# Two mixture-of-experts FFN stages: the order and the waits of GpSimd's row gathers and weight splits

## The chip, the core and the metric
One core of one Trainium2 chip runs the whole kernel as a single program. The metric is the device time in microseconds, lower being better. The time before is the median of three runs, and one further execution was recorded by the hardware profiler. Engines are named as the profile names them: PE is TensorE's matrix unit (PEld its weight load), ACT is ScalarE, DVE is VectorE, POOL is GpSimd, and SP is SyncE, which issues most of the transfers.

## The reference
The input x is 2 sequences of 1024 tokens with 128 features, 2048 tokens in all. Four blocks follow one another, each with a layer norm in front and a residual around it: a selective-scan mixer (a), an FFN, a second state-space mixer (b), and the same FFN again. The FFN is the part that matters here:

```python
def _L0_ffn_ref(x, gate_weight, shared_gate_up, shared_down, experts_gate_up, experts_down):
    E, TOPK, I = 8, 2, 938
    out = _swiglu(x, shared_gate_up, shared_down)          # every token, one shared expert
    probs = softmax(x @ gate_weight.T)
    top_p, sel = top_k(probs, TOPK)                        # two of eight experts a token
    top_p = top_p / (sum(top_p) + 1e-08)
    cw = sum(top_p[..., None] * one_hot(sel, E), axis=2)
    for e in range(E):
        out = out + cw[..., e:e+1] * _swiglu(x, experts_gate_up[e], experts_down[e])
    return out
```
`_swiglu` multiplies silu of a gate projection (128 to 938) by an up projection (128 to 938) and projects back to 128.

## The kernel before
The kernel keeps x transposed in SBUF (128 features by 2048 tokens) and writes the five engines' programs by hand: within a stage each engine runs its own list of instructions, and semaphores order them. `ffn_stage` is built twice, with the prefixes `f_` and `g_` in the names of its tiles.

**Routing.** A stage computes only what the router chose. Its 2 x 2048 (token, expert) pairs are sorted by expert and padded to 39 tiles of 128 slots (`SLOT_TILES = 39`). While the shared expert's first three quarters run on TensorE, VectorE works out which token stands in which slot (`source`), where each result row goes (`back`), its weight (`share`) and a `table` of the expert of each tile.

**Rows.** SyncE stores the normalised tokens as rows in DRAM (`xn_rows`). GpSimd fetches them, 128 rows of 512 bytes for each tile, with an indirect DMA (L1041): gather j fills `rows[:, j, :]` for tile j. Eight semaphores (`GATHERS = 8`) take turns as signals of the landing, `x_loaded[j % 8]`. After tile j has been computed, its results replace the rows, and GpSimd sends them to `token_rows` by a scatter (L1050), waiting at every fourth send until all earlier sends have landed.

**Weights.** Each expert has 1.45 MB of weights, loaded by SyncE in three transfers (L967 to L969) into one of three places of a ring (`RING = 3`). The products are computed in two parts, so GpSimd splits each expert's weights into a rounded high part and the rest: two casts (L1020, L1021) and two subtractions (L1023, L1025), which end with `w_ready`. A split waits for its load (`w_loaded`), and the load of expert n, from the fourth on, waits on SyncE for `summed`, TensorE's count that the last tile of expert n-3 is done:

```python
            for n in range(RING + 1, EXPERTS + 1):
                at = 2 * SLOT_TILES + n - RING
                first = sp.value_load(table[0:1, at:at + 1], min_val=1, max_val=SLOT_TILES)
                sp.wait_ge(summed, first + NPRE)
                load_expert(n)
```

**TensorE's tile.** `tile(j)` turns the gathered rows of tile j (L1200, "turn j" below; it waits for gather j), multiplies the products of tile j-2 by the down weights (`down_tile`, L1185 and L1188), turns the products of tile j-1 (L1167), and then, after `w_ready` of its expert, multiplies the rows by gate and up weights in two halves (L1214 to L1216). ScalarE and VectorE read each of these results from PSUM: ScalarE scales the cross term (L1361), rounds the turned products (L1356) and takes silu (L1379), VectorE multiplies (L1730), subtracts (L1699, L1703) and writes the result rows (L1709). The tiles at which one expert ends and the next begins follow from the routing table, which the inputs fix.

**GpSimd's order.** Split of expert 1; gathers 0 to 3; split 2; gathers 4 to 15; split 3; gathers 16 to 27; split 4; gathers 28 to 38; splits 5 and 6; sends 0 to 3; split 7; sends 4 to 13; split 8; the other sends; at the end four additions of returned rows. Before gather j, from the fifth on, it waits until gather j-4 has landed.

Of the kernel before, what the change touches and what calls it, by code (L numbers as in the profile page):

```python
# [8 lines left out]
F32 = mybir.dt.float32  # L9
F32R = mybir.dt.float32r  # L10
I32 = mybir.dt.int32
ALU = mybir.AluOpType
# [16 lines left out]
EXPERTS = 8  # L29
# [9 lines left out]
RING = 3  # L39
GATHERS = 8  # L40
# [14 lines left out]
class Core:  # L55
# [5 lines left out]
    def sb(self, name, shape, dt=F32, ctx=None):  # L61
        return (ctx or self.ctx).enter_context(self.nc.sbuf_tensor(name, shape, dt))
# [759 lines left out]
def ffn_stage(k, d, which, tag, cleared, ready, out=None, logs=None, following=None):  # L822
# [5 lines left out]
    nc, ps = k.nc, k.ps  # L828
# [4 lines left out]
    def sems(names):  # L833
        made = [k.sem(f"{tag}_{n}", counters) for n in names.split()]
        spent.extend(made)
        return made
# [12 lines left out]
    logit, prob, chosen, rank, spare, place = [sb(n, [P, TT, EXPERTS]) for n in  # L849
                                               "logit prob chosen rank spare place".split()]  # L850
# [24 lines left out]
    x_loaded = k.gathered  # L875

    def gathered(j):
        before = len(range(j % GATHERS, SLOT_TILES, GATHERS))
        return 16 * (j // GATHERS + 1 + which * before)

    w_loaded = sems(" ".join(f"w_loaded{b}" for b in range(RING)))
# [75 lines left out]
    def down_of(ring, place):  # L957
        return ring[:, place, 2 * GW:EW].rearrange("p (i h m) -> p i h m", i=TILES, h=2)

    with stage, nc.Block(no_gpsimd_drain=True) as block:  # L960
# [50 lines left out]
        @block.gpsimd  # L1011
        def _(pool):
            TOGETHER, SEND_FIRST, SEND_SECOND = 4, EXPERTS - 4, TT - 2

            def split_expert(n):
                place = (n - 1) % RING
                high, low, dn = ring[:, place, 0:GW], ring[:, place, GW:2 * GW], down_of(ring, place)
                raw, raw_dn = raw_ring[:, place, GW:2 * GW], down_of(raw_ring, place)
                pool.wait_ge(w_loaded[place], 48 * ((n - 1) // RING + 1))
                nc.gpsimd.tensor_copy(high, raw).then_inc(w_high, 1)  # L1020
                nc.gpsimd.tensor_copy(dn[:, :, 0, :], raw_dn[:, :, 1, :]).then_inc(w_high, 1)  # L1021
                pool.wait_ge(w_high, 2 * n - 1)
                nc.gpsimd.tensor_tensor(low, raw, high.bitcast(F32), ALU.subtract)  # L1023
                pool.wait_ge(w_high, 2 * n)
                nc.gpsimd.tensor_tensor(dn[:, :, 1, :], raw_dn[:, :, 1, :], dn[:, :, 0, :].bitcast(F32),  # L1025
                                        ALU.subtract).then_inc(w_ready, 1)

            split_expert(1)
            pool.wait_ge(k.first_row, 16)
            pool.wait_ge(rows_stored, 16 * TOP * NCH)  # L1030
            pool.wait_ge(source_ready, 1)
            for j in range(SLOT_TILES):
                if j == 4:
                    split_expert(2)
                if j == 16:
                    split_expert(3)
                if j == 28:
                    split_expert(4)
                if j >= TOGETHER:
                    pool.wait_ge(x_loaded[(j - TOGETHER) % GATHERS], gathered(j - TOGETHER))  # L1040
                nc.gpsimd.indirect_dma_start(rows[:, j, :], None, k.xn_rows,  # L1041
                                             bass.IndirectOffsetOnAxis(ap=source[:, j:j + 1], axis=0))\
                    .then_inc(x_loaded[j % GATHERS], 16)
            for n in range(RING + 2, EXPERTS - 1):
                split_expert(n)
            def send(j):
                pool.wait_ge(outs_ready, j + 1)
                if j and j % TOGETHER == 0:
                    pool.wait_ge(sent, sent_before + 16 * j)
                nc.gpsimd.indirect_dma_start(k.token_rows, bass.IndirectOffsetOnAxis(ap=back[:, j:j + 1], axis=0),  # L1050
                                             rows[:, j, :], None).then_inc(sent, 16)

            pool.wait_ge(share_ready, 1)
            for j in range(SEND_FIRST):
                send(j)
            split_expert(EXPERTS - 1)
            for j in range(SEND_FIRST, SEND_SECOND):
                send(j)
            split_expert(EXPERTS)
            for j in range(SEND_SECOND, SLOT_TILES):  # L1060
                send(j)
            for g in range(NCH):
                pool.wait_ge(out_loaded[g], 16 * TOP)
                part = slice(4 * g, 4 * g + 4)
                nc.gpsimd.tensor_tensor(both[:, 0, part, :], both[:, 0, part, :], both[:, 1, part, :], ALU.add)\
                    .then_inc(both_ready, 1)
# [1566 lines left out]
```

## Time and profile before

| | us |
|---|---|
| median of 3 runs (1105.61 to 1109.13) | 1106.93 |
| the profiled execution | 1106.46 |
| its span, first to last instruction | 1104.7 |
| PE busy | 981.6 (89%) |
| DVE busy | 740.1 (67%) |
| POOL busy | 601.3 (54%) |
| ACT busy | 571.5 (52%) |
| 39 gathers of the first FFN (L1041), busy | 37.2 |
| mean granted TensorE clock | 0.957 |

Times inside the profile count from the span's start. The gathers of the first FFN are issued between 328.0 and 413.1, those of the second between 826.4 and 911.1. A POOL row of an indirect DMA is the time in which GpSimd writes the transfer's descriptors; the landing comes later and is seen only in who waits for it. In a row of the timeline the bracket gives the idle time of the engine ahead of the instruction and what ended it: "DMA" or an engine with its line, "issue" where nothing that the profile shows was waited for, "remote" where the releaser is unknown to it.

### The profile page before, as it was taken

Reading aid. Unit: us, or ns where it says so; the run is one execution under the profiler, and the core shown is the slowest. Engines: PE = TensorE matmul, PEld = TensorE weight load, DVE = VectorE, ACT = ScalarE, POOL = GpSimd, SP = SyncE. Lnnn points to the kernel's source line nnn. Section 1 sums busy time; section 2 is a strip of 40 time slices with the busy share of each in tenths; the row PEclk is TensorE's granted clock in tenths of the full one; section 3 lists DMA queues with packets and bytes.
Section 4 is the critical chain, followed back from the end, with each engine's and each line's share of the span. In section 5 each row is a group of like instructions: output and inputs, shape, how many; then the busy total and the mean of one; then the engine's idle time right before and its main releaser. Section 6 shows DMA issues by size and latency. Waiting matters only on the chain. (4 is left out here: it accounts for less than half of the span.)

```text
span 1104.7 us, 16232 instructions
## 1 busy us (share of the span) xinstructions
PE 981.6 (89%) x4715; PEld 693.3 (63%) x4715; DVE 740.1 (67%) x1211; ACT 571.5 (52%) x1109; POOL 601.3 (54%) x467
## 2 busy tenths in 40 slices
PE   6989999998996588999999879979997588999997
PEld 2323333333675578989896446556676577989896
DVE  2899999996784335556566867765794345655565
ACT  6674657664423335545555676766523334545453
POOL 3589888996308673467222747420308773456412
PEclk9999999989998898999999889999999898999999
DMA  4322232332411123220003000001402122222104
GB/s 141 77 70 71 81 87 82 98 99 79 150 41 52 50 58 97 79 75 28 23 13 101 23 0 1 1 1 60 144 21 70 37 72 58 60 72 77 34 13 120
DMA packets 60400, 69.41 MB, mean 63 GB/s; under 512 B 6232, under 2 KB 42848, under 8 KB 60320
## 3 DMA queue, kind: packets, MB, share of 16 engines
q1 hardware_dynamic: 55328, 58.15, 17.6%
q0 software_dynamic: 4992, 10.23, 3.7%
q8 instruction: 46, 0.75, 0.3%
q14 instruction: 34, 0.28, 0.1%
HBM read 57.74 MB, written 10.62 MB: 62 GB/s over the span
## 5 line engine op out<-in xcount | busy, mean ns | idle before, releaser
L795 POOL TENSOR_TENSOR a_hc<-a_h,a_c_sb 128x512 f32<-128x512 f32 x128 | 159.6, 1271 | 27.7 <-DVE a_h L695 27.7
L471 PE MATMUL ps<-a_hc,eye 128*128 128x512 f32 x256 | 135.1, 644 | 9.6 <-POOL a_hc L795 8.9
L610 ACT ACTIVATE ps<-a_delta,a_neg_a 128x512 f32<-128x512 f32 x128 | 87.4, 688 | 70.1 <-DVE a_h L695 67.1
L1185 PE MATMUL ps<-g_ring_rounded,g_q_hi_rounded 128*128 x312 | 81.3, 350 | 19.8 <-DVE g_q_hi_rounded L1703 16.9
L1185 PE MATMUL ps<-f_ring_rounded,f_q_hi_rounded 128*128 x312 | 81.2, 350 | 18.8 <-DVE f_q_hi_rounded L1703 18.8
L471 PEld LDWEIGHTS ps<-a_hc,eye 128*128 128x128 f32 x256 | 45.6, 196 | 77.6 <-POOL a_hc L795 40.6
L695 DVE TENSOR_TENSOR_SCAN a_h<-ps,a_state,a_b_u 128x512 f32<-128x512 f32 x64 | 79.0, 1279 | 1.0 <-ACT ps L610 0.9
L1185 PEld LDWEIGHTS ps<-g_ring_rounded,g_q_hi_rounded 128*128 128x128 f32 x312 | 61.6, 198 | 24.5 <-issue 22.3
L695 DVE TENSOR_TENSOR_SCAN a_h<-ps,a_b_u 128x512 f32<-128x512 f32 x64 | 75.2, 1211 | 2.3 <-ACT ps L610 2.1
L1185 PEld LDWEIGHTS ps<-f_ring_rounded,f_q_hi_rounded 128*128 128x128 f32 x312 | 61.7, 198 | 23.4 <-issue 21.2
L1050 POOL DMA_INDIRECT token_rows<-f_rows,f_back x39 | 38.0, 973 | 63.1 <-DVE f_rows L1709 44.7
L1050 POOL DMA_INDIRECT token_rows<-g_rows,g_back x39 | 38.0, 973 | 58.2 <-DVE g_rows L1709 34.7
L675 DVE TENSOR_TENSOR a_b_u<-a_du,ps 128x1024 f32<-128x1024 f32 x57 | 68.5, 1202 | 0.1
L1730 DVE TENSOR_TENSOR g_prods<-g_work,ps 128x470 f32<-128x470 f32 x78 | 49.5, 644 | 25.7 <-PE ps L1216 14.0
L1730 DVE TENSOR_TENSOR f_prods<-f_work,ps 128x470 f32<-128x470 f32 x78 | 49.6, 644 | 24.9 <-PE ps L1216 11.2
L1041 POOL DMA_INDIRECT g_rows<-xn_rows,g_source x39 | 37.1, 952 | 52.3 <-DVE g_source L1657 41.2
L1041 POOL DMA_INDIRECT f_rows<-xn_rows,f_source x39 | 37.2, 955 | 49.8 <-DVE f_source L1657 38.7
L1214 PE MATMUL ps<-g_ring_rounded,g_work_rounded 128*128 x156 | 62.4, 400 | 1.9 <-issue 1.9
L1214 PE MATMUL ps<-f_ring_rounded,f_work_rounded 128*128 x156 | 62.4, 400 | 1.5 <-issue 1.4
L1020 POOL CAST g_ring_rounded<-g_ring 128x1876 fp32r<-128x1876 f32 x8 | 14.0, 1756 | 91.3 <-DMA g_ring<-in_dn 91.3
L1188 PE MATMUL ps<-f_ring_rounded,f_q_lo_rounded 128*128 x273 | 62.5, 229 | 0.0
L1188 PE MATMUL ps<-g_ring_rounded,g_q_lo_rounded 128*128 x273 | 62.4, 229 | 0.0
(472 smaller groups left out, 2806.1 us busy)
## 6 DMA issues: line engine op xcount, KB each, us to landing
a_c_sb<-c_rows SPq DMA_DIRECT2D x64, 256.0 KB, 3.3
f_ring<-in_gu SPq DMA_DIRECT2D x16, 469.0 KB, 4.4
g_ring<-in_gu SPq DMA_DIRECT2D x16, 469.0 KB, 5.2
f_ring<-in_dn SPq DMA_DIRECT2D x8, 512.0 KB, 6.0
g_ring<-in_dn SPq DMA_DIRECT2D x8, 512.0 KB, 6.9
xn_rows<-f_work SPq DMA_DIRECT2D x8, 256.0 KB, 4.2
f_rows<-token_rows SPq DMA_DIRECT2D x8, 256.0 KB, 4.9
xn_rows<-g_work SPq DMA_DIRECT2D x8, 256.0 KB, 3.9
```

Source lines behind the costliest of these rows:

```text
L471: nc.tensor.matmul(ps[:, Y + f, :], k.eye[:, :], hc[:, s % WAITING, :], start=False, stop=(n == NST - 1)).then_inc(y_added, 1)
L610: nc.scalar.activation(ps[:, A + m % NA, :], delta[:, f, cols(g)], ACT.Exp, scale=neg_a[:, f, n:n + 1])\
L675: nc.vector.tensor_tensor(decayed_in[:, p:p + FT, :], du[:, :, cols(g)], ps[:, B + i % 2, :].unsqueeze(1).to_broadcast([P, FT, CH]), ALU.m ...
L695: nc.vector.tensor_tensor_scan(h[:, s % DEPTH, :], ps[:, A + m % NA, :], decayed_in[:, m % FEED, :], initial, ALU.mult, ALU.add).then_inc( ...
L795: nc.gpsimd.tensor_tensor(hc[:, m % WAITING, :], h[:, s % DEPTH, :], c_sb[:, i % RING, :], ALU.mult)\
L1020: nc.gpsimd.tensor_copy(high, raw).then_inc(w_high, 1)
L1041: nc.gpsimd.indirect_dma_start(rows[:, j, :], None, k.xn_rows, bass.IndirectOffsetOnAxis(ap=source[:, j:j + 1], axis=0))\
L1050: nc.gpsimd.indirect_dma_start(k.token_rows, bass.IndirectOffsetOnAxis(ap=back[:, j:j + 1], axis=0), rows[:, j, :], None).then_inc(sent, 16)
L1185: last = nc.tensor.matmul(ps[:, Y2, 0:2 * P], q_hi[:, j % 2, a], in_ring(place, w, w + 2 * P), start=(i == 0), stop=(i == NI), skip_group_ ...
L1188: nc.tensor.matmul(ps[:, Y2, 0:P], q_lo[:, j % 2, a], in_ring(place, w, w + P), start=False, stop=False, skip_group_check=True)
L1214: nc.tensor.matmul(out, xt[:, 0, j % 2, :], w_hi, start=True, stop=False)
L1730: nc.vector.tensor_tensor(prods[:, j % 2, half * H0:half * H0 + HALVES[half]], gates[:, half, 0:HALVES[half]], ps[:, 2 * half + 1, 0:HALVE ...
```

## The change
Three things differ, all in GpSimd's program of `ffn_stage`, and so in both FFN stages. First, from gather 4 on, GpSimd waits before each even gather until both gathers of the pair before have landed, and before an odd gather it doesn't wait. Second, the splits of experts 3 and 4 are cut into their four instructions (`split_part`): a part each follows gathers 5, 7, 9 and 11 (expert 3), and gathers 17, 19, 21 and 23 (expert 4). Third, the split of expert 5, which came after all gathers, is cut likewise and its parts follow gathers 32, 33, 34 and 35. Splits 1, 2, 6, 7 and 8 and all sends keep their place. No instruction's size changes.

```diff
-            TOGETHER, SEND_FIRST, SEND_SECOND = 4, EXPERTS - 4, TT - 2
-
-            def split_expert(n):
+            PARTS, AT_ONCE, UNDER_WAY, AFTER = 4, 4, 2, (6,)
+            BEHIND = {first + step * part: (n, part) for n, first, step in ((3, 5, 2), (4, 17, 2), (5, 32, 1))
+                      for part in range(PARTS)}
+
+            def split_part(n, part):
                 place = (n - 1) % RING
...
+                if part == 0:
+                    pool.wait_ge(w_loaded[place], 48 * ((n - 1) // RING + 1))
+                    nc.gpsimd.tensor_copy(high, raw).then_inc(w_high, 1)
+                if part == 1:
+                    nc.gpsimd.tensor_copy(dn[:, :, 0, :], raw_dn[:, :, 1, :]).then_inc(w_high, 1)
+                if part == 2:
+                    pool.wait_ge(w_high, 2 * n - 1)
+                    nc.gpsimd.tensor_tensor(low, raw, high.bitcast(F32), ALU.subtract)
+                if part == 3:
+                    pool.wait_ge(w_high, 2 * n)
+                    nc.gpsimd.tensor_tensor(dn[:, :, 1, :], raw_dn[:, :, 1, :], dn[:, :, 0, :].bitcast(F32),
+                                            ALU.subtract).then_inc(w_ready, 1)
...
             for j in range(SLOT_TILES):
-                if j == 4:
+                if j == AT_ONCE:
                     split_expert(2)
-                if j == 16:
-                    split_expert(3)
-                if j == 28:
-                    split_expert(4)
-                if j >= TOGETHER:
-                    pool.wait_ge(x_loaded[(j - TOGETHER) % GATHERS], gathered(j - TOGETHER))
+                if j >= AT_ONCE and j % UNDER_WAY == 0:
+                    for i in range(j - UNDER_WAY, j):
+                        pool.wait_ge(x_loaded[i % GATHERS], gathered(i))
                 nc.gpsimd.indirect_dma_start(rows[:, j, :], None, k.xn_rows,
                                              bass.IndirectOffsetOnAxis(ap=source[:, j:j + 1], axis=0))\
                     .then_inc(x_loaded[j % GATHERS], 16)
-            for n in range(RING + 2, EXPERTS - 1):
+                if j in BEHIND:
+                    split_part(*BEHIND[j])
+            for n in AFTER:
                 split_expert(n)
```

## Rows read from the trace of the kernel before

**Rows 1.** Timeline of PE, turns and one tile: start, length, engine, line, operation, [idle]

```profile
333.70 0.33 PE L1200 MATMUL ps<-eye,f_rows 128*128 128x128 f32 x1 [1.03 <-DMA f_rows<-xn_rows,f_source]
...
349.33 0.27 PE L1200 MATMUL ps<-eye,f_rows 128*128 128x128 f32 x1
...
370.74 0.27 PE L1200 MATMUL ps<-eye,f_rows 128*128 128x128 f32 x1
...
398.82 0.27 PE L1200 MATMUL ps<-eye,f_rows 128*128 128x128 f32 x1
...
401.46 0.46 PE L1214 MATMUL ps<-f_ring_rounded,f_work_rounded 128*128 x1
```

**Rows 2.** Windows: edges, length, busy PE, PEld, DVE, ACT, POOL, PEclk, DMA share

```profile
349.33:424.76 75.43, 50.32 (x289) 45.56 (x288) 27.75 (x60) 23.57 (x51) 49.08 (x41) 0.84 0.27 66
847.66:922.95 75.29, 50.63 (x290) 45.70 (x289) 27.72 (x59) 23.58 (x51) 46.27 (x38) 0.82 0.24 57
456.46:570.72 114.26, 112.12 (x758) 103.67 (x757) 68.47 (x147) 58.49 (x127) 50.98 (x42) 1.00 0.15 47
954.73:1070.54 115.81, 112.69 (x758) 103.71 (x757) 68.50 (x147) 58.58 (x127) 61.17 (x48) 1.00 0.15 47
424.76:456.46 31.70, 31.70 (x217) 29.59 (x216) 19.67 (x42) 17.17 (x37) 18.40 (x9) 1.00 0.17 52
```

**Rows 3.** Timeline of ACT and of SyncE's transfers (SPq), expert loads at L967

```profile
350.93 0.60 ACT L1356 ACTIVATE f_q_hi_rounded<-ps 128x512 fp32r<-128x512 f32 x1 [2.24 <-remote]
...
359.41 0.56 ACT L1379 ACTIVATE f_work<-ps 128x468 f32<-128x468 f32 x1 [6.47 <-remote]
...
383.61 0.33 SPq L967 DMA_DIRECT2D f_ring<-in_gu  x1
383.62 0.37 ACT L1361 ACTIVATE f_work<-ps,f_share 128x128 f32<-128x128 f32 x1 [9.66 <-remote]
...
415.28 0.34 SPq L967 DMA_DIRECT2D f_ring<-in_gu  x1
415.29 0.37 ACT L1361 ACTIVATE f_work<-ps,f_share 128x128 f32<-128x128 f32 x1 [8.32 <-remote]
...
437.38 0.33 SPq L967 DMA_DIRECT2D f_ring<-in_gu  x1
...
463.74 0.33 SPq L967 DMA_DIRECT2D f_ring<-in_gu  x1
...
968.19 0.33 SPq L967 DMA_DIRECT2D g_ring<-in_gu  x1
```

**Rows 4.** Timeline of POOL, gathers and one split in the first FFN, second FFN last

```profile
328.03 1.17 POOL L1041 DMA_INDIRECT f_rows<-xn_rows,f_source  x1 [38.69 <-DVE f_source L1657]
...
342.40 0.98 POOL L1041 DMA_INDIRECT f_rows<-xn_rows,f_source  x1 [0.16 <-issue]
...
357.14 1.76 POOL L1020 CAST f_ring_rounded<-f_ring 128x1876 fp32r<-128x1876 f32 x1
358.83 1.04 POOL L1021 CAST f_ring_rounded<-f_ring 128x1024 fp32r<-128x1024 f32 x1
359.83 4.17 POOL L1023 TENSOR_TENSOR f_ring_rounded<-f_ring,f_ring_rounded 128x1876 fp32r<-128x1876 f32 x1
363.97 2.39 POOL L1025 TENSOR_TENSOR f_ring_rounded<-f_ring,f_ring_rounded 128x1024 fp32r<-128x1024 f32 x1
...
380.31 0.94 POOL L1041 DMA_INDIRECT f_rows<-xn_rows,f_source  x1 [0.30 <-issue]
390.18 1.76 POOL L1020 CAST f_ring_rounded<-f_ring 128x1876 fp32r<-128x1876 f32 x1 [8.92 <-DMA f_ring<-in_dn]
...
412.14 0.95 POOL L1041 DMA_INDIRECT f_rows<-xn_rows,f_source  x1 [0.30 <-issue]
...
840.66 0.98 POOL L1041 DMA_INDIRECT g_rows<-xn_rows,g_source  x1 [0.16 <-issue]
```

**Rows 5.** Timeline of POOL, a send in the first FFN

```profile
512.84 0.97 POOL L1050 DMA_INDIRECT token_rows<-f_rows,f_back  x1 [2.02 <-DMA token_rows<-f_rows,f_back]
```

More of the change, by code:

```diff
@@ L1018, in split_expert @@
                 raw, raw_dn = raw_ring[:, place, GW:2 * GW], down_of(raw_ring, place)
[L1019 to L1026, printed above, removed]
+                if part == 0:
[10 more added lines that the diff above has]
+                                            ALU.subtract).then_inc(w_ready, 1)
+            def split_expert(n):
+                for part in range(PARTS):
+                    split_part(n, part)
             split_expert(1)
```

## Prediction

> **What bounds the kernel now.** I read five views, in this order. First the turns of token rows on TensorE: the transpose at L1200 opens tile j's work, so the distance between two turns is the time of one routed tile. Where nothing disturbs it, a tile takes 5.28 us: from turn 11 at 424.76 to turn 17 at 456.46, six tiles take 31.70 us, with PE busy all 31.70 of it [rows 2]. From turn 3 at 349.33 to turn 11 at 424.76 the first FFN needs 75.43 us for eight tiles, where 8 x 5.28 = 42.24 would do: 33.2 us are lost. In the second FFN, turn 3 at 847.66 to turn 11 at 922.95 is 75.29 us: 33.05 us lost. PE is busy only 50.3 and 50.6 us there, and the mean granted clock falls to 0.84 and 0.82, while it is 1.00 in the windows with a busy PE [rows 1, 2].
>
> Second, GpSimd's timeline over the same stretch. It issues gathers in three unbroken trains of 12, 12 and 11: the first from 342.40 to 357.14, the others ending at 381.25 and 413.09. Each gather is 0.95 us with 0.30 us behind it, and the wait for the landing of gather j-4 never shows: the idle time ahead of them is "issue" [rows 4]. Third, who stands still: ScalarE is idle 6.47, 9.66 and 8.32 us before 359.41, 383.62 and 415.29, each time released by "remote", a source that the profile cannot name [rows 3]. These three moments are 2.27, 2.37 and 2.20 us after the end of the three trains. At two of them SyncE is let go within 0.01 us of ScalarE, to issue a weight load that depends on TensorE's count. The first of these loads, expert 4's, wants tile 3 summed, and that product stands right behind turn 5, at 370.74, thirteen microseconds earlier [rows 1, 3]. So something that TensorE's listeners need (the posting of its counts, or a refill of instructions) does not get through while a train runs, and gets through when the last gather has landed. The trace does not tell which of the two it is; the forecast needs only the coincidence.
>
> Fourth, the loss by train: turn 3 at 349.33 to turn 5 at 370.74 is 21.4 us for two tiles, 10.9 too many, for train 1; trains 2 and 3 share the other 22.3 [rows 1]. Train 1 holds others for 17.0 us (342.40 to 359.41) and costs 10.9, so its first 6.1 us are free. That agrees with ScalarE's first pause by "remote", 2.24 us, which begins at 348.69, 6.3 us into the train [rows 3, 4]. Fifth, the sends at L1050: the same kind of operation, in groups of four, with GpSimd waiting 2.02 us for their landing between the groups [rows 5]. There PE hardly pauses: from turn 17 to turn 38, 21 tiles take 114.26 us, 3.4 us over 21 x 5.28; in the second FFN, 115.81, 4.9 over [rows 2]. That is 0.16 to 0.23 us a tile, against 4.1 in the gather stretch.
>
> **The change, part by part.**
>
> *Waits in pairs.* After the first four gathers and expert 2's split, every pair now waits until both gathers of the pair before have landed. This is the pause that the sends have. Trains shrink from 14.7 us of issue to 2.2, with a landing between. What is the landing? Not shown for a gather alone. Below: the 2.02 us of the sends. Above: gather j starts 4.05 us after the end of gather j-4 (4 x 1.25 - 0.95) and does not wait, so 4.05. I take 2.2, the lower of the three releases behind the trains. A pair is then 0.98 + 0.30 + 0.95 + 2.2 = 4.4 us, of which 2.2 are issue: a duty of one half, where the sends have 4.8 of 6.8. The longest hold is 4.4 us, inside the 6.1 that were free. I therefore take the whole 33.2 + 33.05 = 66.2 us as removable and put back what the sends still lose: 0.2 us a tile for the 14 tiles that now lie beside gathers, 2.8 us a stage.
>
> *What the waits cost GpSimd.* Landing gaps lengthen the gathers, so the weight splits move into them. A split has four parts: 1.76, 1.04, 4.17 and 2.39 us [rows 4]. Placed behind the second gather of a pair, parts 0 and 1 hide in the 2.2 us; part 2 sticks out 2.2 (with its 0.15 us behind it), part 3 0.4. Two loads of 1.45 MB fall among the gathers. The first gather of all shows what that does: it ended at 329.20 beside such a load and its row was turned at 333.70, 4.5 us instead of 2.2, so 2.3 us for each load [rows 1, 4].
>
> Expert 3: ready after pairs 4 to 11, 342.40 + 4 x 4.4 + 2.6 = 362.6, before it was 366.4. Its first tile is no earlier than tile 8: no wait. Expert 4's load follows expert 1's last tile (tile 3, summed right after turn 5, now near 362); load to split took 390.18 - 383.61 = 6.6 us [rows 3, 4], so it is there at 369, and part 0 comes after gather 17, at 373.6: no wait. Ready at 342.40 + 10 x 4.4 + 5.2 + 2.3 = 393.9; tile 12 wants it (expert 3's place was released at 437.38, behind tile 11) at about 349.33 + 9 x 5.28 + 2.6 = 399.5 (the first product with expert weights follows its turn by 401.46 - 398.82 = 2.6) [rows 1]. Hidden, 5.6 us to spare. Before the change it was wanted near 433.
>
> *Expert 5's split, moved from behind the last gather to between gathers 32 and 36.* Fourteen pairs (4 to 31) end at 342.40 + 61.6 + 5.2 + 4.6 = 413.8. Gathers 32 and 33 with parts 0 and 1: 2.2 + 1.8 + 2.2 = 6.2 (part 1 lies in the landing). Gathers 34 and 35 with parts 2 and 3: 2.2 + 4.2 + 2.4 + 0.1 = 8.9. Ready at 428.9. The first tile of expert 5 is 17 (expert 4's place was released at 463.74, behind turn 18, where tile 16 is summed) [rows 3], wanted at 349.33 + 14 x 5.28 + 2.6 = 425.9: late by 3.0 us. In the second FFN everything on GpSimd is 840.66 - 342.40 = 498.26 later, 927.2, and expert 5 starts with tile 18 (release at 968.19, one tile later), 847.66 + 15 x 5.28 + 2.6 = 929.5: not late. This wait runs beside the 2.8 us of residual, since PE comes later by those: first stage 3.8 in all, second 2.8. What stands behind it on GpSimd: gathers 36 to 38, expert 6's split (ready near 444, wanted by tile 22 at 452) and the sends.
>
> *The sends.* GpSimd now finishes expert 6's split about 10 us earlier, PE its tiles about 29 us earlier, so the sends catch up with PE five or so tiles later than at tile 31: 5 x 0.2 = 1.0 us a stage more of their small loss. The 25 sends behind expert 8's split, from about 486 (444 + 5 for four sends + 9.4 for a split + 18.7 for ten sends + 9.4), take 25 x 1.7 = 42 us to 529, and the last result is due near 545, so the tail does not grow.
>
> *The wait instructions and the four calls in place of one* add no datapath work: the same 39 gathers and 32 split operations per stage. The few waits sit in the 0.30 us gaps or in the landing.
>
> **Sum.** 66.2 - (3.8 + 1.0) - (2.8 + 1.0) = 57.6 us gained. The profiled execution is 1106.46 (span 1104.7), 0.5 below the median of the runs, 1106.93. 1106.5 - 57.6 = 1048.9: I say 1049.
>
> **Rivals.**
> *Weights late (0.14).* GpSimd takes the place of the held signals. At the other bound, a landing of 4.05 us, a pair is 6.25 and expert 5 is ready at 342.40 + 14 x 6.25 + 0.6 + 4.6 + 8.0 + 8.9 = 452 instead of 426, 26 us late; in the second stage 950 against 929.5, 21 late. 1106.5 - 66.2 + 47 = 1087. For it: the load's 4.5 us. Against: three train ends at 2.2 to 2.4 and sends at 2.0. Between: 1060 to 1087.
>
> *Half cleared (0.09).* A gap of 2.2 us lets only part of what is held through, and half of the loss stays: 1106.5 - 33 = 1073. For it: ScalarE's pauses grow from 2.24 to 6.47 us within one train, so what is held may be let go piece by piece, and gathers write SBUF where sends read it. Against: the sends, whose pause is no longer and whose duty is higher.
>
> *Nothing held by gathers (0.05).* The pauses are TensorE's own or a slow refill, and merely fall there; the change then moves work on an engine with slack: 1106 +- 3. Against: three pauses of 6 to 10 us, all ending 2.2 to 2.4 us behind a train, and the same loss in the second stage. The Trainium skill (DMA: Bandwidth & Descriptors, "Queues, rings and completion order") says that each DMA engine goes round its queues packet by packet. By that rule a refill or a load waits for one packet of a gather at most, the gathers hold nobody, and this rival would hold; DMA engines are busy only 0.27 of the stretch [rows 2], yet the pauses are there, so the rows speak against it.
>
> *Slower (0.06).* A gap of 2.2 us clears nothing, because only a long silence does. Then the hold runs from 342.40 until GpSimd stops at part 0 of expert 4's split, whose load waits for the same held count: 33.4 us held, 27.3 lost. It returns from 382 to expert 5's part 0 (another 27) and over the last pairs (14): 68 lost for 33 now, twice, 1106.5 + 70 = 1176. It turns on whether one landing pause suffices; the sends say that 2.02 us does.
>
> **How the numbers follow.** Main case 0.66, 1040 (all 66 us back) to 1060 (landing 2.7 us, or twice the residual). Range 1040 to 1075: it takes in the half-cleared case and half of the late weights. 0.3% is 3.3 us, about what tells a change from none here. Faster: 0.66 + 0.14 + 0.09 and a sliver of the last two, 0.89; same 0.05; slower 0.06.
>
> **What would show it.** The turns at L1200 5.3 us apart from turn 3 on, turn 11 near 394 instead of 424.76; no ScalarE pause over 2 us released by "remote"; SyncE's load for expert 4 near 362 instead of 383.61; GpSimd idle about 2 us before every second gather, with a landing as its releaser; the granted clock of the stretch above 0.95. I am wrong if GpSimd's pairs are 6 us apart (then PE waits at the first product of tile 17), or if ScalarE's pauses return in smaller pieces.

## Result and the profile after

The changed kernel takes 1055.33 us (median of 4 runs, 1053.29 to 1056.55) where the kernel before, run beside it, takes 1107.43 (4 runs, 1105.61 to 1109.13). The ratio is 0.9523, with a 95% interval of 0.9498 to 0.9548. The profiled execution of the changed kernel took 1053.29 us, its span 1051.2 against 1104.7, and its mean granted clock 0.972 against 0.957. The prediction was 1049, in a range of 1040 to 1075.

In the seven sessions of this study the same kernel before took 1103 to 1109 us in four, this one among them (called slow placements below), and 1031 to 1033 us in three (quick placements), and one chip, number 8, showed both. Every experiment below says on which it ran.

The windows of the changed kernel, cut at the same turns as [rows 2] (turn 3 to 11 in each FFN; turn 17 to 18 and 18 to 38 of the first; turn 17 to 38 of the second; length, busy PE, PEld, DVE, ACT, POOL, granted clock, DMA share, GB/s):

```profile
350.76:392.99 42.23, 42.23 (x289) 39.50 (x288) 26.24 (x56) 22.88 (x49) 28.03 (x21) 1.00 0.31 95
824.78:866.97 42.19, 42.19 (x289) 39.50 (x288) 26.23 (x56) 22.82 (x49) 29.15 (x22) 1.00 0.26 76
424.68:437.09 12.41, 7.04 (x38) 6.16 (x37) 3.28 (x7) 2.86 (x7) 9.80 (x6) 0.72 0.13 19
437.09:548.55 111.46, 107.81 (x721) 98.84 (x720) 65.31 (x140) 55.82 (x121) 63.72 (x49) 1.00 0.16 50
898.74:1017.05 118.31, 113.63 (x757) 103.75 (x756) 68.49 (x147) 58.26 (x127) 73.27 (x55) 1.00 0.16 49
```

The stretch of 75.43 and 75.29 us is now 42.23 and 42.19, eight tiles at 5.28, with PE busy throughout at a granted clock of 1.00. So all 66 us of the gather stretch came back, and no ScalarE pause there ends by "remote". What is left stands in the last three rows: 12.41 us for the one tile from turn 17, and 5.9 and 7.4 us over 5.28 us a tile behind it.

GpSimd's timeline, and after it SyncE's expert loads with the PE row of the first remaining loss and the ACT row of one pause in the second:

```profile
343.70 0.98 POOL L1049 DMA_INDIRECT f_rows<-xn_rows,f_source  x1 [0.16 <-issue]
...
371.42 0.94 POOL L1049 DMA_INDIRECT f_rows<-xn_rows,f_source  x1 [4.47 <-DMA f_rows<-xn_rows,f_source]
372.67 0.94 POOL L1049 DMA_INDIRECT f_rows<-xn_rows,f_source  x1 [0.30 <-issue]
375.83 0.94 POOL L1049 DMA_INDIRECT f_rows<-xn_rows,f_source  x1 [2.22 <-DMA f_rows<-xn_rows,f_source]
...
413.63 0.94 POOL L1049 DMA_INDIRECT f_rows<-xn_rows,f_source  x1 [4.43 <-DMA f_rows<-xn_rows,f_source]
...
429.44 0.95 POOL L1049 DMA_INDIRECT f_rows<-xn_rows,f_source  x1 [0.16 <-issue]
430.41 2.36 POOL L1032 TENSOR_TENSOR f_ring_rounded<-f_ring,f_ring_rounded 128x1024 fp32r<-128x1024 f32 x1
```

```profile
363.32 0.33 SPq L967 DMA_DIRECT2D f_ring<-in_gu  x1
...
384.45 0.33 SPq L967 DMA_DIRECT2D f_ring<-in_gu  x1
...
405.60 0.33 SPq L967 DMA_DIRECT2D f_ring<-in_gu  x1
...
432.91 0.75 PE L1224 MATMUL ps<-f_ring_rounded,f_work_rounded 128*128 x1 [5.37 <-POOL f_ring_rounded L1032]
...
437.09 0.27 PE L1210 MATMUL ps<-eye,f_rows 128*128 128x128 f32 x1
...
479.51 0.37 ACT L1371 ACTIVATE f_work<-ps,f_share 128x128 f32<-128x128 f32 x1 [3.37 <-remote]
```

A pair starts 4.41 us after the one before it (371.42 to 375.83), with a wait of 2.22 us released by a landing: this is the 4.4 of the sum. Expert 4's load goes out at 363.32 instead of 383.61 [rows 3]. Expert 5's split, however, ends at 430.41 + 2.36 = 432.8, and PE has idled 5.37 us for it; the row at 432.91 lasts 0.75 us, where the first such product of a tile lasts 0.46 at a granted clock of 1.00 [rows 1], and the clock in that window is 0.72. In the sends one ACT pause by "remote" of 3.37 us is left, at 479.51.

### The profile page after: what moved, and what is told of

Its sections match the earlier page's. It is cut to its first block and busy times, and to the rows that moved or that the text cites. A ratio compares the mean times of both kernels' runs of the same rounds, so it can differ in the third digit from the quotient of the medians.

```text
span 1051.2 us, 16268 instructions
## 1 busy us (share of the span) xinstructions
PE 969.9 (92%) x4715; PEld 683.5 (65%) x4715; DVE 740.0 (70%) x1211; ACT 572.6 (54%) x1109; POOL 602.6 (57%) x467
## 5 line engine op out<-in xcount | busy, mean ns | idle before, releaser
L1195 PE MATMUL ps<-g_ring_rounded,g_q_hi_rounded 128*128 x312 | 77.1, 337 | 3.0 <-DVE g_q_hi_rounded L1713 3.0
L1195 PE MATMUL ps<-f_ring_rounded,f_q_hi_rounded 128*128 x312 | 77.1, 337 | 2.5 <-DVE f_q_hi_rounded L1713 2.5
L1389 ACT ACTIVATE f_work<-ps 128x470 f32<-128x470 f32 x78 | 43.7, 565 | 38.4 <-PE ps L1226 37.5
L1195 PEld LDWEIGHTS ps<-g_ring_rounded,g_q_hi_rounded 128*128 128x128 f32 x312 | 58.8, 189 | 6.8 <-issue 4.3
L1195 PEld LDWEIGHTS ps<-f_ring_rounded,f_q_hi_rounded 128*128 128x128 f32 x312 | 58.8, 188 | 6.3 <-issue 3.8
L1389 ACT ACTIVATE g_work<-ps 128x470 f32<-128x470 f32 x78 | 43.5, 565 | 32.8 <-PE ps L1226 28.8
```

What stands on the lines that cost most here:

```text
L1195: last = nc.tensor.matmul(ps[:, Y2, 0:2 * P], q_hi[:, j % 2, a], in_ring(place, w, w + 2 * P), start=(i == 0), stop=(i == NI), skip_group_ ...
L1389: nc.scalar.activation(gates[:, half, 0:HALVES[half]], ps[:, 2 * half, 0:HALVES[half]], ACT.Silu)\
```

## Experiments

In each diff "before" or "after" says what it is cut from.

**The waits alone (from before; quick placement).** What the pairs cost where nothing is held.

```diff
-                if j >= TOGETHER:
-                    pool.wait_ge(x_loaded[(j - TOGETHER) % GATHERS], gathered(j - TOGETHER))
+                if j >= 4 and j % 2 == 0:
+                    for i in range(j - 2, j):
+                        pool.wait_ge(x_loaded[i % GATHERS], gathered(i))
```

> The kernel before with the waits in pairs and nothing else: the splits stay whole behind gathers 15 and 27 and behind the last gather. Theory (what a train of gathers holds is let go when the gathers have landed): the three ScalarE pauses of 6 to 10 us vanish, and the turns come 5.28 us apart until weights are missing. The whole splits of 9.4 us and the pair of 4.4 us then make expert 4 ready near 414 where it is wanted near 400, and expert 5 near 448 where it is wanted near 440: 22 us of new waiting at the first product with expert weights in the first stage, some 17 in the second. 66 back, 39 given away: 1080. Rival (the parts between the gathers do it, the waits nothing): 1107, pauses as before.

Measured 1087.71 us, beside 1033.44 for the kernel before in the same session: ratio 1.0539 (1.0483 to 1.0596). The expectation had taken 1107 as its base and 1080 as the outcome; the outcome is near, but it was reached the other way round, since here there was nothing to win back. Its main part, that the waits alone make ScalarE's pauses vanish, was not tested: this edit never ran on a slow placement. PE's waits for weights, whole run:

```profile
PE ps L1215 <- POOL f_ring_rounded L1025: 25.4, 2, 17.7
PE ps L1215 <- POOL g_ring_rounded L1025: 18.3, 2, 12.1
```

Those 43.7 us were estimated at 39. With the low clock behind each wait, turns 3 to 38 of the two stages lose 52.8 us over 5.28 us a tile, which is nearly all of the 54. So the waits in pairs need the parts: without them GpSimd becomes the bound, which is the rival "weights late" at work.

**The parts alone (from after; run on both placements).**

```diff
-                if j >= AT_ONCE and j % UNDER_WAY == 0:
-                    for i in range(j - UNDER_WAY, j):
-                        pool.wait_ge(x_loaded[i % GATHERS], gathered(i))
+                if j >= AT_ONCE:
+                    pool.wait_ge(x_loaded[(j - AT_ONCE) % GATHERS], gathered(j - AT_ONCE))
```

> The changed kernel with the old waits (landing of gather j-4), the splits in parts as in the change. Theory: the parts break the trains a little, but gathers 12 to 17 and 24 to 32 stay unbroken (7.4 and 11 us), and behind 19 only 1 us lies between, so pauses stay at those places: half of the 66 us at most comes back, 1075 to 1095. Rival (the interleaved parts are what helps): 1055, as the change.

On a quick placement: 1030.57 us beside 1033.44, ratio 0.9986 (0.9969 to 1.0002). It says nothing on the pauses, as none were there to remove, and so neither of the two outcomes named above was tested.

> The changed kernel with the old waits (landing of gather j-4) and the splits in parts. Where the kernel before took 1033 us this took 1030.6; this run counts where it takes 1106. The spaced gathers showed there no pause with one gather in 2.4 us and no wait for a landing. If so the parts, of which each puts 1.0 to 4.2 us between two gathers, may do the work alone. Theory now (what counts is how many gathers come back to back; some five or six are free): only the trains of 5 and 6 (gathers 12 to 17, 24 to 32 with a gap where a place is awaited) can hold anything: at most 5 us a stage, and without the landing waits expert 5 is in time (it was ready behind gather 35 at 409.5, wanted at 426): 1042 to 1052, as good as the change or better. Rival (each pair must have landed, parts of 1 us are no gap): half of the 66 us stays, 1065 to 1090.

On a slow placement: 1053.20 us (1049.95 to 1058.21) beside 1103.33, ratio 0.9544 (0.9509 to 0.9580). The whole change has 0.9523 and 0.9515; the intervals overlap. The parts alone thus bring as much as parts and waits, against the first expectation (1075 to 1095) and 1 us over the second (1042 to 1052), but leave their loss in another place, as the trace shows. GpSimd's train of nine gathers (24 to 32), ScalarE's pauses beside it, and the window of turn 11 to 12:

```profile
388.23 0.96 POOL L1048 DMA_INDIRECT f_rows<-xn_rows,f_source  x1 [0.16 <-issue]
...
398.32 0.95 POOL L1048 DMA_INDIRECT f_rows<-xn_rows,f_source  x1 [0.31 <-issue]
399.27 1.76 POOL L1024 CAST f_ring_rounded<-f_ring 128x1876 fp32r<-128x1876 f32 x1
```

```profile
393.92 0.60 ACT L1365 ACTIVATE f_q_hi_rounded<-ps 128x512 fp32r<-128x512 f32 x1 [1.80 <-remote]
396.77 0.60 ACT L1365 ACTIVATE f_q_hi_rounded<-ps 128x512 fp32r<-128x512 f32 x1 [2.24 <-remote]
...
401.08 0.56 ACT L1388 ACTIVATE f_work<-ps 128x468 f32<-128x468 f32 x1 [3.04 <-remote]
```

```profile
394.58:406.95 12.37, 8.41 (x37) 7.45 (x36) 5.53 (x11) 4.56 (x9) 11.09 (x9) 0.72 0.14 37
```

Nine gathers back to back (388.23 to 399.27) cost 12.37 - 5.28 = 7.1 us, and ScalarE is let go at 401.08, 1.8 us behind the last of them. Its first two pauses ended at 393.92 and 396.77, inside the train: so a train delays what ScalarE waits for by some 2 us at first and by more towards its end, and does not simply stop it. A train of six in the second stage, with three more gathers behind it after pauses of 1.2 and 2.1 us, cost 6.0 us (turn 11 to 12, 11.29 us), trains of five cost 1.7 and 1.6 (turn 6 to 7, 6.97 and 6.85 us), and turn 14 to 15, behind a train of three, took 0.75 us too long. In the kernel before twelve cost 10.9, and pairs, in the change, cost nothing. Against this, expert 5 was in time.

The same run shows how short a gap can be. The gathers behind the first two parts of expert 3's split:

```profile
347.86 0.97 POOL L1048 DMA_INDIRECT f_rows<-xn_rows,f_source  x1 [0.17 <-issue]
349.14 0.94 POOL L1048 DMA_INDIRECT f_rows<-xn_rows,f_source  x1 [0.30 <-issue]
350.08 1.05 POOL L1026 CAST f_ring_rounded<-f_ring 128x1024 fp32r<-128x1024 f32 x1
351.30 0.97 POOL L1048 DMA_INDIRECT f_rows<-xn_rows,f_source  x1 [0.17 <-issue]
```

Six gathers (343.70 to 353.52) with gaps of 1.9 and 1.2 us between the pairs cost nothing: turns 2 to 6 stay 5.25 to 5.28 us apart, where five gathers back to back cost 1.6. Both gaps are shorter than the 2.2 us of a landing.

**Spaced gathers (from before; run three times, since the placement could not be chosen).** A pause between gathers without a wait for a landing. The addition's result is used by nobody.

```diff
+    spacer = sb("spacer", [P, 480])
+    spaced, = sems("spaced")
...
                     .then_inc(x_loaded[j % GATHERS], 16)
+                if j >= TOGETHER:
+                    if j > TOGETHER:
+                        pool.wait_ge(spaced, j - TOGETHER)
+                    nc.gpsimd.tensor_tensor(spacer[:, :], k.sh_gu[:, 0, 0:480].bitcast(F32), k.sh_gu[:, 0, 480:960].bitcast(F32), ALU.add)\
+                        .then_inc(spaced, 1)
```

> The kernel before with its old waits, and one GpSimd addition of 480 columns (about 1.1 us, its result unused) behind each gather from the fifth on. GpSimd's pace is then that of the change, one gather in 2.3 us, but a gather lands 2.2 us after it is issued, so one is always under way and the queue is never empty. Theory (only an empty queue clears): the pauses stay and grow with the trains, which last 27 us instead of 15: 1130 or more. Rival (the rate of gathers is what matters, a duty of a half is low enough): the pauses vanish and only late weights are left, about 1080 as with the waits alone.

> The spaced gathers again (old waits, an addition of 1.1 us behind each gather, one gather in 2.37 us, never an empty queue). Where the kernel before took 1033 us it ran in 1083.5 with no pause, all its loss being late weights. This run counts where the kernel before takes 1107. Theory (only an empty queue lets through what is held): pauses by remote of 10 us and more at each train, the turns from 3 on break up, 1110 or more. Rival (a lower rate of gathers is enough): no pause, the same turns as before, 1083 to 1090.

> The spaced gathers a third time, since chips on which the kernel before takes 1033 us (two so far) cannot tell the theories apart. Where it takes 1107: theory (only an empty queue lets through what is held) says pauses by remote of 10 us and more at each train and 1110 us or more; the rival (a lower rate is enough) says no pause and 1083 to 1090. Where it takes 1033: 1083.5 as before, and nothing is learned but that the chip counts.

The first two ran on quick placements: 1083.54 us beside 1033.44 (ratio 1.0504, 1.0468 to 1.0539) and one run of 1083.47 beside 1032.38. The third, one run, ran on a slow one: 1092.69 us beside 1105.88. Its GpSimd rows, its window from turn 3 to 11, and all of ScalarE's waits between 342 and 445 us:

```profile
347.15 0.96 POOL L1043 DMA_INDIRECT f_rows<-xn_rows,f_source  x1 [0.16 <-issue]
348.14 1.23 POOL L1049 TENSOR_TENSOR f_spacer<-sh_gu_rounded 128x480 f32<-128x480 f32 x1
349.53 0.95 POOL L1043 DMA_INDIRECT f_rows<-xn_rows,f_source  x1 [0.16 <-issue]
```

```profile
349.30:393.19 43.89, 42.45 (x290) 39.48 (x289) 26.23 (x56) 22.85 (x49) 41.24 (x35) 1.00 0.32 90
```

```profile
ACT f_work L1386 <- PE ps L1223: 30.3, 17, 16.9
ACT f_work L1368 <- PE ps L1192: 18.9, 13, 1.5
ACT f_work L1368 <- issue: 4.4, 3, 1.5
ACT f_work_rounded L1373 <- PE ps L1207: 2.5, 14, 0.2
ACT f_work L1386 <- issue: 1.4, 2, 0.7
ACT f_work_rounded L1373 <- issue: 0.4, 2, 0.2
```

A gather comes every 2.37 us, and none waits for a landing (0.16 us, "issue"). No wait is by "remote". The window is 43.89 us, 1.65 over 8 x 5.28, of which 1.44 is one wait for expert 3's weights; the rest of what this run loses comes later, the most of it as late weights (turn 12 to 13 takes 23.15 us). The rival, a lower rate, gave 1083 to 1090 and was 3 us too low; the theory gave 1110 or more and pauses, and failed. Its reason, that only an empty queue lets through what is held, is not refuted by this run alone: a gather lands some 2.2 us behind its issue, and the next one's issue ends 2.4 us behind it, so the queue is empty or nearly so for an instant even here. The gaps of 1.9 and 1.2 us in the parts alone speak against it. What is shown is that the wait is not needed and that 1.4 us between gathers are enough.

**128 fulfilled waits on TensorE (from before; twice, both on quick placements).**

```diff
+            if which == 0:
+                for _ in range(128):
+                    pe.wait_ge(k.cent_set, 1)
             for c in range(ready, NCH):
                 centre(c)
```

> The kernel before with 128 waits that are already fulfilled at the head of TensorE's list in the first FFN, so that its later instructions stand half a refill block (256 instructions) further on. Theory in its refill form (a pause starts when a refill of instructions falls into a train): TensorE's refill, now seen between 345 and 348, moves by 128 instructions, about 8 us, so the first pause inside train 1 starts earlier or later by that much, the loss of train 1 changes from 10.9 us by 3 us or more, and the total moves by several us either way. Rival (the train alone holds, whatever is fetched): pauses start 6 us into each train as before and the time is 1107 plus at most 5 for the waits themselves.

> The kernel before with 128 fulfilled waits more on TensorE, so that its refills of instructions fall half a block elsewhere. This run counts where the kernel before takes 1107. Refill form of the theory: a pause starts a few microseconds behind the refill packet that falls into a train, wherever that is; with refills half a block (about 8 us of tiles) away, the loss of train 1 changes from 10.9 us by 3 us or more. Rival (the train alone holds): each train's loss stays within 2 us of 10.9, 12.3 and 10.1, pauses start some 6 us into each train, 1107 plus the 10 us that the waits cost where nothing was held (1042 for 1033).

Measured 1041.94 us beside 1033.44 (ratio 1.0096, 1.0061 to 1.0130), and one run of 1040.81 beside 1032.38. The 8.5 us are put down to the waits themselves: in the second run turn 0 comes at 342.80 us, in the kernel before at 333.70 [rows 1], and behind it nothing is lost. The question of the refills was not answered, because neither run met a slow placement. The traces were worth having all the same: they are the profile of the old gather loop where nothing is held. From the second run, its windows (turn 3 to 11, turn 17 to 38), the first train on GpSimd, and SyncE and ScalarE behind turn 5:

```profile
358.37:400.58 42.21, 42.21 (x290) 39.49 (x288) 26.21 (x56) 22.83 (x49) 36.70 (x28) 1.00 0.35 101
432.29:543.10 110.81, 110.81 (x757) 103.65 (x756) 68.81 (x147) 59.91 (x127) 52.91 (x44) 1.00 0.16 50
```

```profile
351.35 0.98 POOL L1041 DMA_INDIRECT f_rows<-xn_rows,f_source  x1 [0.16 <-issue]
352.63 0.95 POOL L1041 DMA_INDIRECT f_rows<-xn_rows,f_source  x1 [0.30 <-issue]
...
365.13 0.94 POOL L1041 DMA_INDIRECT f_rows<-xn_rows,f_source  x1 [0.30 <-issue]
366.06 1.78 POOL L1020 CAST f_ring_rounded<-f_ring 128x1876 fp32r<-128x1876 f32 x1
```

```profile
370.92 0.33 SPq L967 DMA_DIRECT2D f_ring<-in_gu  x1
370.93 0.37 ACT L1364 ACTIVATE f_work<-ps,f_share 128x128 f32<-128x128 f32 x1 [1.45 <-PE ps L1185]
```

The train is the same as in [rows 4]: twelve gathers, 351.35 to 366.06, 0.94 us each and 0.30 between. Yet eight tiles take 42.21 us with PE busy all the time, ScalarE waits 1.45 us for tile 3's product where it waited 9.66, and expert 4's load, which wants the same count, goes out at 370.92, 2.0 us behind turn 5 and before the next train. Turns 17 to 38 take 110.81 us, 5.28 a tile, so the small loss beside the sends is gone too.

Beside these rows, the kernel before on its slow placement can say more on what is held. There turn 5 stood at 370.74, and TensorE went on as follows:

```profile
372.40 0.33 PE L1185 MATMUL ps<-f_ring_rounded,f_q_hi_rounded 128*128 x1
...
374.42 1.09 PE L1167 MATMUL ps<-eye,f_prods 128*128 128x128 f32 x8 [1.68 <-issue]
...
378.69 0.27 PE L1200 MATMUL ps<-eye,f_rows 128*128 128x128 f32 x1
```

The row at 372.40 is the last product of tile 3, the one that counts `summed` up. TensorE then did all its matmuls up to turn 6 at 378.69, yet ScalarE and SyncE, which both waited for that count, moved only at 383.62 and 383.61 [rows 3], 10.9 us late. The same happens behind turn 9: its last product starts at 405.78, turn 10 at 410.93, and the two listeners move at 415.29 and 415.28. So at these two places it was not a refill of TensorE's own instructions that was missing. A count that arrives late explains both listeners; refills of ScalarE and SyncE that end within 0.01 us of each other, twice, would be the rival, and no run excludes it.

**The changed kernel again, and with expert 5's parts early (slow placement, one session).**

```diff
-            BEHIND = {first + step * part: (n, part) for n, first, step in ((3, 5, 2), (4, 17, 2), (5, 32, 1))
+            BEHIND = {first + step * part: (n, part) for n, first, step in ((3, 5, 2), (4, 17, 2), (5, 25, 2))
```

> The changed kernel again, beside the kernel before on the same chip as it happens to be. In the last runs the kernel before took 1033 us instead of 1107, and its trains of 12 gathers (in the copy with 128 extra waits on TensorE) held nobody: every turn from 3 to 38 came 5.28 us apart. Theory (what the change gives is only what the trains hold up, and that depends on where the program runs): where the kernel before takes 1033, the changed kernel has nothing to win and pays for expert 5's late weights, 5 to 7 us in the first stage: 1037 to 1042, slower by 0.5 to 1%. Where it takes 1107, the changed kernel takes 1055. Rival (the change wins everywhere, and the last runs were a quirk of their edits): at least 40 us faster than the kernel before, whichever that is.

> The changed kernel with expert 5's four parts behind gathers 25, 27, 29 and 31 instead of 32 to 35. Its load has landed near 391, gather 25 is issued near 399, so no part waits, and two of them lie in the landing of a pair. Ready near 421 instead of 432.8, wanted at 427.7: TensorE's wait of 5.4 us before tile 17 and the low clock behind it are gone. Theory: 6 to 7 us less than the changed kernel on the same chip, all of it between turns 17 and 18 of the first stage. Rival (some other load or split is late next, expert 6's): less than 3 us.

The changed kernel: 1053.30 us beside 1108.72, ratio 0.9515 (0.9483 to 0.9547). With the parts early: 1042.81 (1039.76 to 1048.92), ratio 0.9417 (0.9373 to 0.9460). The medians lie 10.5 us apart, the two profiled spans (1048.5 and 1041.3) 7.2, where 6 to 7 were expected; four runs each do not tell which is nearer. Windows of the second, turn 3 to 11 and 17 to 38, and the last two parts of expert 5's split:

```profile
350.24:392.45 42.21, 42.21 (x290) 39.47 (x289) 26.22 (x56) 22.85 (x49) 27.90 (x20) 1.00 0.33 95
424.13:540.85 116.72, 112.94 (x757) 103.67 (x756) 68.59 (x147) 58.69 (x127) 67.62 (x53) 1.00 0.17 50
```

```profile
411.38 4.25 POOL L1029 TENSOR_TENSOR f_ring_rounded<-f_ring,f_ring_rounded 128x1876 fp32r<-128x1876 f32 x1
...
418.02 2.41 POOL L1032 TENSOR_TENSOR f_ring_rounded<-f_ring,f_ring_rounded 128x1024 fp32r<-128x1024 f32 x1
```

The split ends at 420.4 and no tile waits. What is left over 5.28 us a tile, 116.72 - 110.88 = 5.8 us, stands beside the sends.

**Sends in pairs as well (from the version with early parts; twice, both on quick placements).**

```diff
-                if j and j % TOGETHER == 0:
+                if j and j % UNDER_WAY == 0:
```

> The changed kernel with expert 5's parts early and the sends in pairs too (before every second send, wait for all earlier ones). On a chip where the kernel before takes 1107: the sends in fours cost the tiles 23 to 35 some 6 to 8 us a stage over 5.28 us a tile; in pairs they cost none, like the gathers: 1042.8 less 10 to 14, 1030. Rival (the sends' losses are not theirs, or the pairs make them late for the last additions): 1040 to 1050. On a chip where it takes 1033: nothing to win, 1030 to 1035.

> The changed kernel with expert 5's parts behind gathers 25 to 31 and the sends in pairs, once more. On a chip with the kernel before at 1103 to 1109 us: the version with the early parts alone took 1042.8 there, and its sends in fours still cost 6.0 and 7.4 us in turns 17 to 38 over 5.28 us a tile. Theory (a train of four holds a little, a pair nothing): these 13 us go too, turns 17 to 38 take 110.9 us in each stage as on the quiet chips, 1030 to 1035. Rival (the sends' loss does not come from their trains, or later sends hold up the last additions): 1040 or more. On a quiet chip, 1034 as before.

1033.85 us beside 1032.38 and 1033.56 beside 1031.06, each with ratio 1.0008 (0.9986 to 1.0030). So the waits in pairs, on gathers and sends, cost nothing there once the parts are early enough. What they bring on a slow placement could not be tried.

## Why the prediction was right, point by point

**The mechanism: right in what it does, wrong in its condition.** The prediction took from three coincidences [rows 3, 4] that a train of gathers holds up what TensorE's listeners need, and that this ends when the train does. The change confirms the first (66 of 66 us came back), and trains of 2, 5, 6, 9 and 12 gathers cost 0, 1.6, 6.0, 7.1 and 10.9 us on slow placements (six and nine were seen once each, and the second train of twelve in the kernel before cost 12.2). The second holds for the longest pauses only; shorter ones end inside a train, as that of 2.24 us before 350.93 does [rows 3]. That the gap must contain a landing was an assumption, and the parts alone speak against it, with gaps of 1.9 and 1.2 us that lost nothing. So the whole gain was credited to the waits in pairs, while the parts, counted only as cover for their cost, bring as much alone (0.9544); that the sum came out all the same is in part luck. "The first 6.1 us are free" was too generous: a train of five has 5.9 us of issue and still cost 1.6. And on a quick placement no train holds anything, which nothing in one profile could have said.

**The rival "nothing held by gathers" (0.05)** was given 1106 and is wrong where it was asked. The Trainium skill (DMA: Bandwidth & Descriptors, "Queues, rings and completion order") lets each DMA engine take its queues in turn, packet by packet. Where the old loop loses nothing (42.21 us for eight tiles), the trace is in keeping with this; where it loses 33 us a stage, the same trains of the same length hold others for up to 10 us, and no run shows whether what is held passes through a DMA queue at all.

**The pair: 4.4 us** predicted, 4.41 measured, with the landing wait at 2.22.

**Late weights of expert 5: the mis-sized term.** Predicted 3.0 us late, measured 5.37, plus 1.8 us of low clock behind it, 7.1 in all. The sum has 3.8 for this wait and the residual together, and its own terms give no more than 3.0, since the two run side by side; the other 0.8 is not derived. The step that failed is "two loads of 1.45 MB fall among the gathers". There are three before gather 32: at 363.32, 384.45 and 405.60. The third, expert 6's, follows tile 11, which the prediction's own pace put near 404. It makes the gather at 413.63 wait 4.43 us instead of 2.2. The split ended 3.9 us later than the sum's 428.9; 1.3 of it is the later start of gather 4 (343.70 for 342.40), which turn 3 shares (350.76 for 349.33), and most of the rest is this load. In the second stage, where expert 5 begins with tile 18, it cost nearly nothing (turn 18 to 19 in 5.42 us), as predicted.

**The residual beside the gathers: 2.8 us a stage** predicted, none measured: turns 3 to 17 of the first stage take 73.92 us, 14 x 5.28.

**The sends: +1.0 us a stage** predicted, +2.5 measured (turns 17 to 38 lost 3.4 and 4.9 before, and lose 5.9 from turn 18 and 7.4 now). All of it is gone on quick placements, and the pause of 3.37 us ends at 479.51, 0.9 us behind a train of four sends. So trains of four seem not to be free on a slow placement, and GpSimd now runs more of them beside PE; sends in pairs, the run that would show it, never met a slow one.

**The sum.** By turns 3 to 38 the first stage gained 221.39 - 197.79 = 23.6 us, the second 222.88 - 192.27 = 30.6, together 54.2, where 57.6 were predicted. The first stage: 7.1 us for expert 5 instead of 3.8 for it and the residual (measured at nothing), -3.3, and 2.5 for the sends instead of 1.0, -1.5. The second: no residual, +2.8, and the sends, -1.5. That is -3.5 of the -3.4. The spans differ by 53.5, the medians by 52.1.

**Open.** What is held, TensorE's counts or a refill of instructions, was not settled by a run; the one for it met only quick placements, and the trace of the kernel before excludes only a refill of TensorE's own at two of the pauses. Whether a train stops what is held or only lets it through more slowly than it comes is open too; pauses that grow from 2 to 10 us within a train speak for the second. The waits alone on a slow placement are untested. What makes a placement slow or quick is unknown. The changed kernel itself was not timed on a quick one: from expert 5's 7.1 us it should be slower than the kernel before there, by an estimate of at most 0.7% (7.1 of 1033), and the version with early parts and paired sends is measured level.

## What to carry to other kernels

When an engine stands still for a releaser that the profile cannot name, line up the ends of its pauses with the other engines' rows: here three pauses ended 2.2 to 2.4 us behind the last of a train of GpSimd's DMAs, and acting on it was worth 5%, though what is held is still not known. Fill the gaps of such a train with work that GpSimd has to do anyway, and count every transfer that the new, faster pace pulls into the stretch, not those that were there before. And run the kernel before in each session anew: a gain measured in one place may only remove a loss of that place.

## What the runs showed of the hardware

All on slow placements unless said otherwise. A pause of 1.4 us between GpSimd's indirect DMAs (one in 2.37 us instead of one in 1.25) removed all pauses by "remote" that ScalarE had beside them, without any wait for a landing (one run). The same gather loop, back-to-back gathers of 0.94 us with 0.30 between, held TensorE's listeners for up to 9.7 us on a slow placement and for nothing on a quick one; the kernel before is 72 to 78 us apart between the two, 7%. In the longest of these pauses TensorE ran on while two listeners of one of its counts moved together, 10.9 us behind the product that counts. Beside a load of 1.45 MB the wait for a pair of gathers to land was 4.4 to 4.5 us instead of 2.2. In the tile with a PE wait of 5.4 us for weights the granted clock was 0.72, at a cost of 1.8 us beyond the wait.
